# Four layers on one core: a first output sum ahead of a low half on VectorE, and a residual behind two low halves on GpSimd

## What is computed

```python
x = x + _layernorm(_L0_attn_ref(_layernorm(x, axis=-1), L0_attn_wq, L0_attn_wk, L0_attn_wv, L0_attn_wo), axis=-1)
x = x + _layernorm(_L0_ffn_ref(_layernorm(x, axis=-1), L0_ffn_gate_w, L0_ffn_gate_scale, L0_ffn_up_w, L0_ffn_up_scale, L0_ffn_down_w, L0_ffn_down_scale), axis=-1)
x = x + _layernorm(_L1_attn_ref(_layernorm(x, axis=-1), L1_attn_wq, L1_attn_wk, L1_attn_wv, L1_attn_wo), axis=-1)
x = x + _layernorm(_L1_ffn_ref(_layernorm(x, axis=-1), L1_ffn_in_gamma, ...), axis=-1)
```

```python
def step(kv, inp):
    qi, ki, vi = inp
    scores = jnp.einsum('bhid,bhjd->bhij', qi, ki) * diag[None]
    o_intra = jnp.einsum('bhij,bhje->bhie', scores, vi)
    o_inter = jnp.einsum('bhid,bhde->bhie', qi * q_dec[None, :, :, None], kv)
    kv = blk[None, :, None, None] * kv + jnp.einsum('bhjd,bhje->bhde', ki * k_dec[None, :, :, None], vi)
    return (kv, o_intra + o_inter)
...
q = _rope(q)
k = _rope(k)
...
return jnp.einsum('bse,de->bsd', o, wo)
```

## Time and profile before

| | us |
|---|---|
| median of 3 runs | 3982.33 |
| lowest and highest | 3981.26, 3989.48 |
| the profiled execution | 3974.35 |
| its span, first to last instruction | 3972.6 |
| PE busy in it | 3646.9 |
| DVE busy | 2539.0 |
| ACT busy | 1506.6 |
| Pool busy | 1455.5 |

### The profile page before, as it was taken

One profiled execution on the slowest core, in us unless ns is written; L12 is line 12 of the kernel. 1 busy time (PEld: TensorE's weight loads), 2 busy tenths in 40 slices (PEclk: granted clock), 3 DMA queues, 4 the chain that ended last, 5 costly groups with the idle time before them and its releaser, 6 DMA issues.

```text
span 3972.6 us, 51225 instructions
## 1 busy us (share of the span) xinstructions
PE 3646.9 (92%) x18536; PEld 2679.4 (67%) x18536; DVE 2539.0 (64%) x4046; ACT 1506.6 (38%) x2349; POOL 1455.5 (37%) x1802
## 2 busy tenths in 40 slices
PE   7878899999999999999999999999999999977678
PEld 5656776687767776687767776687767776654323
DVE  6754676567765677567664776567765676466347
ACT  4423433434252434434243424334243434315124
POOL 3421452245323552245323542245323552232114
PEclk8989999999999999999999999999999999987789
DMA  6556533254324533254325433353325342332303
GB/s 244 176 198 253 210 137 137 98 196 168 133 94 159 189 117 139 102 213 147 128 102 186 169 110 140 131 195 127 145 94 206 139 154 86 117 109 84 129 25 145
DMA packets 173799, 579.00 MB, mean 146 GB/s; under 512 B 14727, under 2 KB 14983, under 8 KB 168174
## 3 DMA queue, kind: packets, MB, share of 16 engines
q1 hardware_dynamic: 169854, 568.38, 39.8%
q10 hardware_dynamic: 3696, 7.34, 0.5%
HBM read 490.21 MB, written 84.93 MB: 145 GB/s over the span
## 4 chain that ended last, share of the span: by engine, by line
PE 55%; DVE 22%; issue 9%; POOL 5%; ACT 4%; DMA 4%; SPq 0%; DVEq 0%; ACTq 0%; POOLq 0%
PE ps_P L1928 20%; PE ps_Y L1928 9%; PE ps_E L1928 6%; PE ps_O L1928 4%; PE ps_O L2165 3%; PE ps_T L2134 2%; PE ps_T L1928 2%; DVE roped L1390 2%; DVE pf L1449 2%; PE ps_E L2148 2%; DVE row_max L1593 2%; DVE ps_T L1586 2%; POOL X L864 1%; DVE stats L1356 1%; DMA w_big<-split_dram 1%
## 5 line engine op out<-in xcount | busy, mean ns | idle before, releaser
L1928 PE MATMUL ps_P<-XnT_hi,w_ring 128*128 128x512 f32 x3328 | 1070.7, 403 | 40.4 <-DVE hf L1613 10.8
L1928 PEld LDWEIGHTS ps_P<-XnT_hi,w_ring 128*128 128x128 f32 x3328 | 599.5, 189 | 209.5 <-issue 76.2
L1928 PE MATMUL ps_P<-XnT_lo,w_ring 128*128 128x512 f32 x1664 | 653.3, 393 | 0.0
L979 POOL TENSOR_TENSOR hT_lo<-hf,hT_hi 128x512 fp32r<-128x512 f32 x128 | 164.5, 1285 | 910.8 <-ACT hT_hi L1045 910.8
L1197 ACT ACTIVATE probs<-ps_E 128x1024 f32<-128x1024 f32 x320 | 328.4, 1026 | 437.1 <-PE ps_E L2148 436.2
L871 POOL TENSOR_TENSOR pT_lo<-pf,pT_hi 128x512 fp32r<-128x512 f32 x256 | 344.4, 1357 | 362.2 <-ACT pT_hi L1045 362.2
L1593 DVE TENSOR_REDUCE row_max<-ps_T 128x2 fp32r<-128x768 f32 (+3 forms) x448 | 400.2, 917 | 11.0
L1586 DVE TENSOR_TENSOR ps_T<-ps_T,mask 128x512 f32<-128x512 f32 (+1 forms) x320 | 188.3, 589 | 307.6 <-PE ps_T L2134 306.2
L1928 PE MATMUL ps_Y<-w_big,hT_hi 128*128 128x512 f32 x896 | 335.1, 418 | 32.4 <-POOL hT_lo L979 19.6
L1928 PEld LDWEIGHTS ps_P<-XnT_lo,w_ring 128*128 128x128 f32 x1664 | 314.2, 189 | 69.7
L1045 ACT ACTIVATE pT_hi<-pf 128x512 fp32r<-128x512 f32 x256 | 160.7, 632 | 342.2 <-DVE pf L1449 341.9
(11 more groups left out here) (330 smaller groups left out, 7359.0 us busy)
## 6 DMA issues: line engine op xcount, KB each, us to landing
w_ring<-split_dram SPq DMA_DIRECT2D x412, 512.0 KB, 3.4
w_big<-split_dram SPq DMA_DIRECT2D x64, 2048.0 KB, 7.7
dec<-decay SPq DMA_DIRECT2D x32, 1024.0 KB, 5.0
split_dram<-w_ring SPq DMA_DIRECT2D x58, 512.0 KB, 4.3
split_dram<-w_big SPq DMA_DIRECT2D x36, 512.0 KB, 4.3
wo1w<-split_dram SPq DMA_DIRECT2D x8, 2048.0 KB, 7.6
gatew<-split_dram SPq DMA_DIRECT2D x7, 2048.0 KB, 10.9
X<-raw_f SPq DMA_DIRECT2D x46, 256.0 KB, 4.3
```

The costliest lines, as they stand in the source:

```text
L979: pool.tensor_tensor(hT[1][:, m % IC, :], hf[:, m % 2, :], hT[0][:, m % IC, :].bitcast(F32), ALU.subtract).then_inc(*h_lo.hit(n, m))
L1928: last = pe.matmul(dst, stat[s_], mov[m_], start=first_ and k == 0, stop=last_ and k == n - 1, **kw)
```

## The change

Two moves, and nothing is added or taken away. On DVE `accumulate(n, g - 1, 0)` goes from the head of `blocks` (for `g` of 1 and more) to the end of `rope`, ahead of the last unit's low half. On Pool the fourth residual goes into `blocks(n, 0)`, ahead of job 2, for every batch but the first. The last round, which has no group of heads, keeps its own order.

```diff
             def blocks(n, g):
                 for k in range(2 if g else 0, NJOB):
+                    if k == 2 and g == 0 and n:
+                        residual("qb", resid_b, n - 1, NT - 1, X[(n - 1) % 2][:, NT - 1, :], y_acc[:, NT - 1, :])
                     if k < NRING:
                         job_low(n, g, k)
...
                     for t in range(NT):
                         rstds("qb", c, t)
-                    for t in range(NT):
+                    for t in range(NT - 1):
                         residual("qb", resid_b, c, t, X[c % 2][:, t, :], y_acc[:, t, :])
...
+                if g:
+
+                    accumulate(n, g - 1, 0)
                 rope_low(n, g, NU - 1)
...
                 else:
-                    accumulate(n, g - 1, 0)
                     accumulate(n, g - 1, 1)
                     state_low(n, g)
```

## The result

The changed kernel takes **3926.57 us** (median of 4 runs, 3922.42 to 3930.11), beside 3983.06 us for the kernel before (median of 4, 3981.26 to 3989.48). The ratio is 0.9856, with a 95% interval of 0.984 to 0.9872: faster by 1.4%, or 56 us. The forecast was 3927 us, with a range of 3914 to 3950. The profiled execution took 3927.53 us, 46.8 us less than the profiled one before.

The account below looks back on a forecast made before the run. PE, busy 92% of the span, and its waits were taken to bound the kernel. Gains of 29.4 + 1.2 + 6.9 + 14.4 = 51.9 us gave 3922.4 or 3930.4 us; the middle, 3927 us, was forecast, range 3914 to 3950.

Parts of the forecast that it names:

- place 1, 21 places: First sum ahead of the low half on DVE, batches 2 to 8: PE's wait shrinks 1.4 us each, 29.4 us.
- first batch: The same move at three places of the first batch: 0.8 us each, bounds 0 and 2.4 us, taken 1.2 us.
- place 2, batches 3 to 8: Fourth residual behind two low halves on Pool; DVE's multiply starts 0.02 us first: 1.1 us a batch, 6.6 us.
- place 2, batch 2: The same residual move in batch 2, where PE comes late and waits only 0.16 us: 0.3 us.
- clock: Nine stretches of half clock behind PE's waits, batches 2 to 8, taken as gone: 1.6 us each, 14.4 us.
- The 8 us: Median 8.0 us above the profiled execution: 3930.4 us if it stays, 3922.4 if it goes; the middle, 3927, taken.
- Pool first: Rival at place 2: Pool starts before DVE's multiply, gain 1.5 instead of 6.9 us, two low stretches stay; 3936 us, chance 0.16.
- The low clock is not won back: Rival: low stretches fall elsewhere, 14.4 us not gained; 3945 us, or 3950 with Pool first as well; chance 0.17.
- PE waits for something else: Rival at place 1: PE waits for its own queue or the state product, not the copy; 3975 to 3985 us, chance 0.03.
- The slower rival: Low clock moves into the attention stage's 67 row-maxima waits, 1.6 us each; 3993 us with 30 stretches; chance 0.02.

Follow-up runs that it names:

- experiment 1: The kernel before with only the first sum moved ahead of the last unit's low half, the four residuals staying together: 3933.53 us, ratio 0.9876.
- experiment 4: The kernel before with the state's low half put ahead of the first two sums, so the first sum comes later: 4005.73 us, ratio 1.0054.
- experiment 5: The changed kernel with one unused DVE bn_stats ahead of the moved sum, so PE waits 0.87 us: 3941.02 us, ratio 0.9889.
- experiment 6: The changed kernel with an unused bn_stats and an unused maximum on DVE ahead of the moved sum, PE waiting 1.20 us: 3946.79 us, ratio 0.9916.
- experiment 3: Both kernels again, nothing edited, for second profiles: changed kernel 3926.3 us, ratio 0.9854; kernel before, one run, span 3984.6 us.
- experiment 8: The changed kernel with an unused bn_stats of 128 columns ahead of DVE's multiply for job 1, so Pool starts before that multiply: 3933.51 us, ratio 0.9882.
- experiment 7: The changed kernel with a tiny unused DVE memset ahead of the multiply for job 1; DVE still started first: 3924.11 us, ratio 0.9847.
- experiment 9: The changed kernel with the first sum one instruction earlier, ahead of the last unit's rotation: 3909.27 us, ratio 0.981; in another job 3908.32 us, ratio 0.9819.
- experiment 2: The kernel before with only the fourth residual moved behind the low halves of jobs 0 and 1: 3968.89 us, ratio 0.9964.

## Why the prediction was right

The time came out within 0.5 us of the forecast, and the mechanism was the one named. Term by term, against the profiled executions (predicted 51.9 us, measured 46.8):

| term | predicted | measured |
|---|---|---|
| place 1, 21 places | 29.4 | 29.4 (39.4 to 38.0 us a group) |
| first batch | 1.2 | -0.5 (opening of batch 2, 416.7 to 417.2 us) |
| place 2, batches 3 to 8 | 6.6 | 6.6 (51.7 to 50.6 us) |
| place 2, batch 2 | 0.3 | 0.0 (45.9 to 45.9 us) |
| clock | 14.4 | 14.4 (9 to 0 stretches) |
| not in the sum | 0 | -3.1 |

- **Place 1** held in every step: the copy in the gap, the low half not late, 0.26 us left. The sum went by one group's rows and multiplied; that was safe because all 21 waits were alike. Experiments 1, 4, 5 and 6 show that the distance of the groups follows this wait one to one, in both directions.
- **The first batch** came out 0.5 us below its bounds, and the term can't be read from these two profiles. The three waits shrank as said, from some 1.98 to 1.19 us (the earlier trace rows and the row below), and the second and third group each stand 0.6 us nearer to the next (44.5 to 43.9 us, 44.4 to 43.8 us). But from the fourth group to batch 2 it took 245.7 us before and 249.7 us after. That can't be laid to the change: the second profile of the kernel before (experiment 3) has 249.3 us there and opens batch 2 at 418.8 us, later than both profiles of the changed kernel (417.2 and 416.7 us). PE's timeline after; then the window of the first feed-forward layer, which waits for raw weights, of the kernel before in its first and second profile, and after:

```profile
142.75 0.47 PE L1932 MATMUL ps_Y<-w_big,oT_hi 128*128 128x512 f32 x1 [1.20 <-DVE y_acc L1431]
```

```profile
220.00:416.00 196.00, 157.71 (x634) 120.88 (x633) 98.55 (x159) 56.19 (x95) 33.35 (x42) 0.92 0.64 242
```

```profile
220.00:416.00 196.00, 156.37 (x619) 119.75 (x618) 98.46 (x159) 55.56 (x94) 31.99 (x39) 0.91 0.64 241
```

```profile
220.00:416.00 196.00, 159.56 (x622) 122.44 (x623) 95.75 (x153) 55.83 (x95) 30.12 (x36) 0.90 0.64 243
```

  The clock falls from 0.92 to 0.91 without any change. What makes this stage take 246 or 249 us stays open.
- **Place 2** held, by its 0.02 us. The choice of the likelier case by the rows 883.87 to 884.64 of the earlier trace rows (Pool starts 0.14 us behind ACT) was right in six of six batches, and experiment 8 shows what hung on it: 7 to 11 us. The term for batch 2 was nothing, since PE's small wait there was not the last.
- **The clock** was the boldest term. Two profiles of the changed kernel with no low stretch, and none at the 21 waits of 0.87 us and the 21 of 1.20 us, bear it out.
- **Not in the sum**: in batch 6 PE waited 1.28 us for the load of w_big in the last group (0.28 us before), which is 1.0 us. Six other profiles have one such wait of 0.89 to 1.52 us in batch 6 or 7, and in two of them the four residuals stand together as before (0.98 us in experiment 1, 1.20 us in experiment 4), so it can't be laid to the second move. From the last group to the end 2.3 us were lost (the gain of the last place counted), and 0.2 us came back elsewhere. That part took 778.5 and 781.3 us in the two profiles of the kernel before, so this too is within what it varies by.
- **The 8 us** between profile and median: I took the middle for want of knowing. In experiment 3 the differences between executions are mostly low stretches, and those went. If all 8 us were such, the time is 3922.4 plus the 5.1 us of the table that did not come, 3927.5 for the profiled execution. That the midpoint met the median is thus partly two errors that cancel: 4.5 us kept that went, 5.1 us counted that did not come.

The rivals: Pool first did not come by itself, and was about right in price when forced (the prediction puts its gain at 1.6 us in one place and at 1.5 in another). "The low clock is not won back" and "PE waits for something else" have no sign in either profile. The slower rival rested on a view of the whole span, and its sentence that all of these waits run at full clock today is not so. Cut to the stretch from batch 2 to the last group, the waits for the row maxima before are these:

```profile
PE ps_T L2134 <- DVE row_max L1593: 19.4, 36, 0.9
```

None is over 0.9 us; the ones of up to 2.2 us stand in the last round, where the page's slices show a clock of 7 to 9 tenths anyway. With 36 waits of at most 0.9 us, and no low stretch behind waits of 0.87 us in experiment 5, that rival had less for it than the prediction said.

## What to carry to other kernels

A fixed order on an engine can hold an instruction whose input was ready microseconds ago behind one that waits for a third engine. Look for the idle gap ahead of the blocking one, put the ready one into it, and then ask whether it could stand one place earlier still; here that second step brought 14 to 17 us more. Price a wait of the busiest engine at its own length times its places, and where low clock stands behind it, add that. Take two profiles of the same kernel before reading a difference of a few microseconds in one stage: here one stage took 246 or 249 us, with the change and without it. Where two engines exclude each other, hundredths of a microsecond decide who pays, so read both starts, not only durations.

## What the runs showed of the hardware

**Low clock behind short waits.** From batch 2 to the end of the last group, low stretches behind PE's waits, by the length of the wait:

| wait, us | which | low stretches |
|---|---|---|
| 0.28 | the moved sum, five profiles (changed kernel twice, experiments 1, 7, 8) | 0 of 105 |
| 0.87 | experiment 5 | 0 of 21 |
| 1.12 to 1.15 | hT_lo, each profile | 0 of 6 each |
| 1.20 | experiment 6 | 0 of 21 |
| 1.20 to 1.29 | w_big, experiments 4 and 7 and the changed kernel | 0 of 3 |
| 1.36 to 1.38 | pf, experiment 8 | 3 of 6 |
| 1.52 to 1.62 | pf, four profiles (before twice, experiments 1 and 4) | 7 of 24 |
| 1.52 | w_big, experiment 9, second profile | 1 of 1 |
| 1.65 to 1.68 | the sum, before twice and experiment 2 | 24 of 63 |
| 2.25 to 2.27 | experiment 4 | 12 of 21 |

Each stretch shows as half clock, of the 2.4 GHz that PE otherwise has, and costs 1.6 us, about as much as the wait ahead of it. DVE ended all of the longer waits but one; that one was ended by a DMA, and low clock stands behind it too. These are its rows (PE's timeline, then the window):

```profile
2296.52 0.50 PE L1931 MATMUL ps_Y<-w_big,oT_hi 128*128 128x512 f32 x1 [1.52 <-DMA w_big<-split_dram]
```

```profile
2297.00:2300.40 3.40, 3.40 (x10) 2.62 (x9) 1.27 (x1) 0.12 (x1) 2.40 (x2) 0.50 0.00 0
```

I had expected the share to rise with the length of the wait. From 1.67 to 2.25 us it did not: one execution of the kernel before had 13 of 21, that of experiment 4 had 12. But the cases are not independent. The low stretches at the place of the sum come in runs within a batch: in batches 4 and 6 of the first profile of before, and 3, 4 and 7 of the second, all three places were hit, and in batches 2, 5, 7 and 8 of the first none. So the shares of the rows from 1.36 us on are rough. What the table does show is that the 42 waits of 0.87 and 1.20 us, at the same places, had none.

**The exclusion of DVE and Pool does not take every instruction.** In experiment 8 DVE's bn_stats (one input) started 0.02 us ahead of Pool's low half and did not stretch it (1.29 us). The multiply behind it (two inputs) was held: it ended at 873.47 + 1.66 = 875.13, that is 0.55 us behind Pool's end at 874.58. It was so in all of batches 3 to 8, but the bn_stats took only 0.28 us, so there was little to stretch.
